# Attention kernel of two layers: which transpositions stand ahead of the output projection's portions, and in which parts a batch's normalisation is prepared

## What is computed

```python
xn = layernorm(x)
q, k, v = xn @ Wq + bq, xn @ Wk + bk, xn @ Wv + bv        # 16 heads of 64
q, k = rope(q), rope(k)
attn = softmax(causal(q @ k.T / 8))                       # 512 x 512 for each head
x = x + (attn @ v) @ Wo + bo + int8_linear(xn)            # attention + quantised linear layer
xn = layernorm(x)
left, right = xn @ compare_left, xn @ compare_right
c = left @ right.T / 16
x = x + ((c > threshold) * softmax(c + gate_bias)) @ xn + rwkv_ffn(xn)
```

## Time and profile before

| | us |
|---|---|
| median of 3 runs | 1048.55 |
| lowest, highest | 1047.62, 1048.55 |
| the profiled execution's time | 1048.61 |
| its span on the core | 1046.8 |
| PE busy | 997.9 (95%) |
| DVE, ACT, POOL busy | 846.8, 758.2, 766.6 |

### The profile page before, as it was taken

The page is one execution under the profiler, slowest core; times in us unless marked ns, Lnnn a source line. Parts: engine busy times, 40 slices in busy tenths (PEclk is TensorE's granted clock), DMA queues, the critical chain, the costliest instruction groups (busy, mean ns, idle before and its releaser), DMA issues.

```text
span 1046.8 us, 23671 instructions
## 1 busy us (share of the span) xinstructions
PE 997.9 (95%) x7974; PEld 673.3 (64%) x7974; DVE 846.8 (81%) x2272; ACT 758.2 (72%) x2014; POOL 766.6 (73%) x941
## 2 busy tenths in 40 slices
PE   5878998999999999999999999999999998999998
PEld 4545555666666666666666666666666765777776
DVE  7979889877878888877787777877787766998875
ACT  5968887666666767766666676666666766999994
POOL 3766667868787877787787878777867645878884
PEclk9989999999999999999999999999999999999999
DMA  8723444343333343234333333433333100000101
GB/s 273 231 82 112 142 132 134 92 132 92 111 108 92 97 117 99 90 114 119 92 92 111 92 97 91 122 97 91 99 101 96 52 1 1 22 22 21 34 30 41
DMA packets 99703, 98.70 MB, mean 94 GB/s; under 512 B 13312, under 2 KB 95360, under 8 KB 98944
## 3 DMA queue, kind: packets, MB, share of 16 engines
q1 hardware_dynamic: 99584, 97.19, 30.4%
HBM read 56.25 MB, written 40.90 MB: 93 GB/s over the span
## 4 chain that ended last, share of the span: by engine, by line
PE 71%; DVE 15%; ACT 7%; issue 4%; POOL 2%; DMA 1%; ACTq 0%; DVEq 0%; SPq 0%; POOLq 0%
PE bank L1640 22%; PE bank L1723 13%; PE bank L1737 12%; PE bank L1754 7%; PE bank L1711 6%; PE bank L1712 5%; PE bank L1929 2%; ACT arena L869 2%; PE bank L1875 1%; DVE arena L1516 1%; POOL arena L628 1%; DVE arena L1362 1%; DVE arena L1378 1%; DVE arena L1340 1%; DVE arena L1342 1%
## 5 line engine op out<-in xcount | busy, mean ns | idle before, releaser
L628 POOL TENSOR_SCALAR arena<-arena,rc 128x128 f32<-128x128 f32 (+3 forms) x512 | 275.4, 556 | 198.2 <-DVE rc L1371 198.2
L869 ACT ACTIVATE arena<-arena,nm 128x256 f32<-128x256 f32 (+3 forms) x512 | 283.4, 554 | 74.5 <-DVE nm L1362 69.1
L1362 DVE CUSTOM_DVE_ANT_0 arena<-bank,mask_rows 128x256 f32<-128x256 f32 (+3 forms) x512 | 232.9, 482 | 79.0 <-PE bank L1712 78.4
L1723 PE MATMUL bank<-ident,arena 128*128 128x128 f32 x1280 | 222.7, 280 | 20.1 <-DVE arena L1378 14.4
L1723 PEld LDWEIGHTS bank<-ident,arena 128*128 128x128 f32 x1280 | 149.1, 140 | 87.6 <-DVE arena L1378 52.1
L877 ACT ACTIVATE arena<-bank 128x512 f32<-128x512 f32 (+3 forms) x256 | 108.5, 424 | 65.6 <-PE bank L1723 65.5
L1737 PE MATMUL bank<-arena 128*64 128x512 f32 (+3 forms) x1024 | 153.1, 441 | 0.0
L1712 PE MATMUL bank<-arena 128*128 128x256 f16 (+3 forms) x512 | 152.9, 299 | 0.0
L1711 PE MATMUL bank<-arena 128*128 128x256 f16 (+3 forms) x512 | 139.9, 300 | 1.9 <-DMA arena<-scr 1.9
L1378 DVE COPY arena<-bank 128x512 f32<-128x512 f32 (+3 forms) x256 | 124.8, 487 | 20.6 <-PE bank L1723 16.8
L1737 PEld LDWEIGHTS bank<-arena 128*64 128x64 f32 x1024 | 68.1, 137 | 96.0 <-issue 71.6
(11 more groups left out here) (173 smaller groups left out, 2201.6 us busy)
## 6 DMA issues: line engine op xcount, KB each, us to landing
arena<-scr SPq DMA_DIRECT2D x320, 128.0 KB, 2.7
scr<-arena SPq DMA_DIRECT2D x256, 128.0 KB, 1.7
arena<-in_weights SPq DMA_DIRECT2D x5, 1024.0 KB, 7.5
x_sb<-in_x SPq DMA_DIRECT2D x8, 512.0 KB, 8.6
out<-x_sb SPq DMA_DIRECT2D x16, 256.0 KB, 2.2
xscr<-arena SPq DMA_DIRECT2D x12, 256.0 KB, 3.0
xsh<-xscr SPq DMA_DIRECT2D x6, 256.0 KB, 3.6
xsl<-xscr SPq DMA_DIRECT2D x6, 256.0 KB, 4.1
```

The costliest lines, as they stand in the source:

```text
L628: last = pool.tensor_scalar(pr[slot][:, OFF[i]:OFF[i + 1]], pr[slot][:, OFF[i]:OFF[i + 1]], rc[:, slot, i:i + 1], 1.0, ALU.mult, ALU.mult)
L869: act.activation(pr[slot][:, OFF[i]:OFF[i + 1]], pr[slot][:, OFF[i]:OFF[i + 1]], ACT.Exp, scale=-1.0, bias=nm[:, slot, i:i + 1], accum_out ...
L1362: dve.tensor_tensor_reduce(pr[slot][:, OFF[i]:OFF[i + 1]], s_tile[i], mask_rows[:, SQ - P * (i + 1):SQ], -1.0, -MASKED, ALU.add, ALU.min, ...
L1723: last = pe.transpose(banks[5 + h][:, (i - j) * P:(i - j + 1) * P], pr[2 * par + h][:, OFF[i] + j * P:OFF[i] + (j + 1) * P], ident[:])
```

## The change

Six edits, all of them in the order or the placing of instructions. No product is added or removed but for the fill.

1. PE: `pt(n, 0, 1)` goes ahead of `ffn`, `attended` and `columns_of_rows(n, 0)`; `pt(n, 2, 0)` and `pt(n, 2, 1)` go ahead of the second half's `attended` and `columns_of_rows(n, 1)`.
2. DVE: the roots of batches 1 to 7 are done in four parts: the first guess at the end of ring -1, steps 1 and 2 in the first gap of ring 0, step 3 with `roots_bias` and `bvs` in its second gap. The estimate lies in PSUM bank `wo` until the last step, and the step's three operations are written in another order, so that each reads it once.
3. DVE: `row_maximum(0)` goes to the end of ring 0, `row_maximum(1)` to the first gap of ring 1, the four `part_maximum` to rings 1 to 4, one each (before: rings 1 and 2 one each, ring 3 two); `column_maximum` and `weight_scale` of ring 5's second gap, `low_part(0..3)` and `quantise(0, 1..3)` of rings 8 to 10 go from the gaps to ring ends. ACT's `normal_rows(1)` in ring 0 is split like those of the later rings.
4. POOL: the memset of `kz[1]` goes behind the scaling of the tables.
5. PE: the 50 fill products of 128 columns ahead of ring -2's `evens` become 80 of 64 columns.
6. End: the last batch's last `av3` runs bank by bank, and the first `final` waits for the first bank alone.

```diff
--- POOL
             last.then_inc(diag_done, 1)
-            pool.memset(kz[1], 0.0).then_inc(kz_zero, 1)
 
             pool.wait_ge(setup_done, 1)
...
                 last.then_inc(tab_done, 1)
+            pool.memset(kz[1], 0.0).then_inc(kz_zero, 1)
--- ACT, ring
-                if 1 <= n < NB - 1:
+                if 0 <= n < NB - 1:
                     normal_rows(n + 1, (0,))
...
-                    normal_rows(n + 1, (2, 3) if n else range(NT))
+                    normal_rows(n + 1, (2, 3))
--- DVE
-            def root_step(s, base, r, y0, t1, t2):
-
-                dve.tensor_tensor(t2, y0, y0, ALU.mult).then_inc(s, 1)
+            def root_step(s, base, r, y0, t1, t2, out):
+
+                dve.tensor_tensor(t2, y0, t1, ALU.mult).then_inc(s, 1)
                 dve.wait_ge(s, base + 4 + 3 * r)
-                dve.scalar_tensor_tensor(out=t2, in0=t2, scalar=-0.5, in1=t1, op0=ALU.mult, op1=ALU.mult).then_inc(s, 1)
+                dve.scalar_tensor_tensor(out=t2, in0=t2, scalar=-0.5, in1=y0, op0=ALU.mult, op1=ALU.mult).then_inc(s, 1)
                 dve.wait_ge(s, base + 5 + 3 * r)
-                dve.scalar_tensor_tensor(out=y0, in0=t2, scalar=1.5, in1=y0, op0=ALU.add, op1=ALU.mult).then_inc(s, 1)
+                dve.scalar_tensor_tensor(out=out, in0=t2, scalar=1.5, in1=y0, op0=ALU.add, op1=ALU.mult).then_inc(s, 1)
...
             def first_gap(n):
 
-                if 0 <= n < NB and n != 1:
+                if n == 0:
+                    roots(later_tiles, 1, (1, 2), wo)
+                elif n < NB and n > 0:
                     row_maximum(n)
...
-                elif n == 8:
-                    low_part(0)
-                elif n == 9:
-                    quantise(0, 1)
-                elif n == 10:
-                    low_part(2)
...
                 elif n == 0:
-                    dve.wait_ge(act_stats, NB - 3)
-                    inverse_roots(slice(1, NB), 1)
+                    roots(later_tiles, 1, (3,), wo)
+                    roots_bias(later_tiles)
                     dve.tensor_scalar(bvs[:], vec[:, V_BV:V_BV + NP], inv[:, G_V:G_V + 1], None, ALU.mult)
-                elif 1 <= n <= 3:
-                    if n == 1:
-                        row_maximum(1)
+                elif 1 <= n <= 4:
                     part_maximum(n - 1)
-                    if n == 3:
-                        part_maximum(3)
-                elif n == 5:
-                    column_maximum(slice(G_O, G_L), 2)
-                    weight_scale(slice(G_O, G_L), 2)
+                elif n == 6:
                     dve.tensor_tensor(sc_vo[:], sc[:, G_V:G_V + 1], sc[:, G_O:G_O + 1], ALU.mult)
-                elif n == 8:
-                    low_part(1)
-                elif n == 9:
-                    quantise(0, 2)
-                elif n == 10:
-                    low_part(3)
...
             def ring_end(n):
 
-                if n == 7:
+                if n == 0:
+                    row_maximum(0)
+                elif n == 5:
+                    column_maximum(slice(G_O, G_L), 2)
+                    weight_scale(slice(G_O, G_L), 2)
+                elif n == 7:
                     quantise(0, 0)
+                    low_part(0)
                 elif n == 8:
                     input_scale()
+                    low_part(1)
                 elif n == 9:
-                    quantise(0, 3)
+                    for step in range(1, 4):
+                        quantise(0, step)
+                elif n == 10:
+                    low_part(2)
+                    low_part(3)
...
                 odd_terms(n + AHEAD)
+                if n == -1:
+                    dve.wait_ge(act_stats, NB - 3)
+                    roots(later_tiles, 1, (0,), wo)
                 inverse(n + 1, 1, e)
--- PE, ring
                 scores(n + 1, 0, (0, 2))
+                pt(n, 0, 1, o)
                 if n == NP + 2:
                     ffn(0, 0, wo)
...
                 if 1 <= n < NB:
                     columns_of_rows(n, 0)
-                pt(n, 0, 1, o)
                 scores(n + 1, 0, (3,))
...
                 scores(n + 1, 1, (1,))
+                pt(n, 2, 0, o)
+                pt(n, 2, 1, o)
                 if n == NP + 2:
                     attended(0, 0, (0, 1, 2), wo)
...
                     columns_of_rows(n, 1)
-                pt(n, 2, 0, o)
-                pt(n, 2, 1, o)
                 scores(n + 1, 1, (0, 2))
--- PE, fill and end
-            FILL = (0, 60, 0, 50)
+            FILL = (0, 60, 0, 40)
+                for _ in range(count):
+                    for a, z in ((identb, maskb), (maskb, identb)):
+                        pe.matmul(pt1[:, 0:L], a[:], z[:, 0:L], start=True, stop=True)
...
+            def av3_by_bank(n, j, par):
+
+                after(pe, pt3l_done, made(4, n, j))
+                for w in range(2):
+                    av3_terms(j, par, (2 * w, 2 * w + 1)).then_inc(av3_mm, 1)
```

## The result

The changed kernel takes 1032.74 us in the median (1031.76 to 1034.57), against 1048.1 for the kernel before measured beside it: a ratio of 0.9856, with an interval of 0.9838 to 0.9873. Forecast was 1028.0, a gain of 20.6; the gain is 15.4.

The account below looks back on a forecast made before the run. PE paces the rings, so a step saves time only where PE waits or runs at a low clock. From 1048.6, -11.2 + 0.5 - 5.05 - 3.35 - 0.8 - 0.7 = -20.6 gives 1028.0 us, range 1024.8 to 1032.8.

Parts of the forecast that it names:

- The steady wait: Rings 12 to 59: transpositions ahead of the projection remove PE's wait for DVE's copy; -11.2 us, bounds 0 and 17 saved.
- rival (a): Saving given back at the next copy: the wait at pt(n,3,1) grows from 0.14 to 0.39; 1039 us, chance 0.07.
- The other 44 save 0.25: Of the 48 rings from 12 to 59, all but rings 25 to 28 save 0.25 us each, 11.0 in sum.
- rival (c): In 52 rings the projection gets stuck behind POOL's normalise(n,1) at pt(n,0,1); slower, 1065 us, chance 0.03.
- Rings 60 to 63: Waits of 0.1 to 0.75 for POOL's normalise at pt(n,0,1), against 0.25 saved in each; +0.5 us in sum.
- Moving `pt(n,2,h)` 0.65 ahead: Needs ACT's copy of key tile 1; costed at nothing, gain only 0.04 us in rings with n % 4 == 0.
- Ring 0 and the start: Roots in parts and PE's clock staying up, -5.05 us; faster first root and weight maxima at the start, -0.8.
- the hidden guess: The roots' first guess at ring -1's end, hidden where DVE waits 0.9 us for ACT's sums and POOL is idle.
- Rival (b) in its second form: Ring 0's clock falls at 1.5 us of idling all the same, +2.6; 1030.6 us, chance 0.22 for either form.
- The memset beside the low parts: POOL's memset beside Wq's low parts at the start costs nothing, since it only writes SBUF; upper bound 1.8 us.
- Rings 1 to 9: DVE work moved out of gaps shortens PE's waits; -3.35 us including rings 10 and 11, bounds -1.5 and -4.5.
- The end: First bank's six products and final need not wait for the other bank's six; -0.7 us, bounds 0 and -0.8.

Follow-up runs that it names:

- `first_only`: The changed kernel with pt(n,2,0) and pt(n,2,1) back behind the projection's portion, pt(n,0,1) still ahead; 1031.91 us, ratio 0.9847.
- `pe_only`: The kernel before with the PE order alone changed (both moves of the transpositions), nothing else; 1040.01 us, ratio 0.9927.
- `roots_sbuf_b`: The changed kernel with the roots' estimate in SBUF instead of PSUM, same four places, second run for a clean profile; 1034.75 us, ratio 0.9872.
- `after`: The changed kernel itself, with all six edits, against the kernel before; 1032.74 us, ratio 0.9856.
- `second_only`: The changed kernel with pt(n,0,1) back behind the projection, pt(n,2,0) and pt(n,2,1) still ahead; 1043.16 us, ratio 0.995.

## Why the prediction was off by 4.7

By the profiled executions the forecast was off by 5.1, in these parts.

- **The steady wait, -11.2 forecast, -9.1 found.** The mechanism was right: 0.24 in most rings with n % 4 not 0 (12.43 to 12.19), from the first move alone, with the next copy shifting along, so rival (a) fell. The step that failed is the count: "The other 44 save 0.25", with 0.4 taken off for rings with one-off work. Rings 20, 23, 58 and 59 gave nothing and ring 22 gave 0.17; in rings 23 and 58 the wait at `pt(n,3,1)` comes from DVE's one-off work, and it grew by as much as was saved (ring 58: from 0.52 to 0.81 by the spacing of the products). Ring 59 has no `evens` any more and belongs with the next item. Ring 29 lost 0.23, since POOL's normalise was late in it and the projection stood behind: rival (c) in one ring. The ten rings with n % 4 == 0 gave 0.22 and not 0.29. I had taken 0.4 off for all this; it is 2.5.
- **Rings 60 to 63, +0.5 forecast, +2.06 found.** Here the failed step is "Moving `pt(n,2,h)` 0.65 ahead ... I cost it at nothing". I had checked ACT's copy in a ring with `evens`. In rings 59 to 63 no `evens` stand between the transpositions of tile 1 and those of tile 2, only scores and the projection, and the second move takes the projection out of the way too. So PE comes to tile 2 before ACT's and DVE's copies of tile 1 are done (in ring 61 the loads wait 0.31 and 0.20, in ring 60 PE itself 0.30): 1.6, shown by `first_only`. The +0.5 for POOL's normalise was right (0.45).
- **Ring 0 and the start, -5.85 forecast, -6.02 found.** The waits of `roots_bias` and `bvs`, the hidden guess and the clock that stays up at a short wait came as worked out, and from the V product to ring 1 it is 19.13 - 14.17 = 4.96 less, for the 5.05 forecast. PE's wait was 0.77, below the 1.5 forecast. That the sum agrees within 0.2 is in part luck on both sides. The maxima ended 1.2 earlier and not 0.8, and the first stretch of the changed kernel is 68.3 to 71.3 in the twelve profiles with the roots in parts and in PSUM, all with the same DVE work in ring 0. And 1.0 of the 4.96 is the long fall in the profile of the kernel before, as `pe_only` shows; I read one execution's fall as the kernel's. Rival (b) in its second form (the clock falls at 1.5 of idling) didn't come true in ring 0. The falls at the two earlier waits cost 0.1 to 1.0 and not its 2.6.
- **The memset beside the low parts.** It cost nothing (4.48 and 4.48), so the rule of the Trainium skill ("SBUF — State Buffer", section "Who interferes with whom"), that two SBUF inputs contend with a GpSimd instruction that reads SBUF and not with one that only writes it, agrees with the trace. The trace agrees for readers too: 0.84 to 0.91 beside the scaling of the tables, and Newton steps of 0.4 to 1.2 in SBUF beside normalise and `rotate` against 0.19 with one operand in PSUM. Two steps with SBUF inputs at the start of normalise took 0.18 and 0.19 all the same; why isn't shown.
- **Rings 1 to 9, -3.35 forecast with rings 10 and 11, -2.72 found.** Rings 3, 4 and 5 went as forecast (-0.58, +0.60, -1.36), and rings 8 and 9 too (-1.14 for -1.2). Ring 1 gave 1.12 and not 0.6, which hid most of the next miss. Ring 6's +0.68 was missed: I read the `sc_vo` move as a cost of nothing. A DVE operation on two SBUF columns has no cost of its own worth booking, but waits out the POOL instruction beside it, which is what the forecast said of `roots_bias` and failed to say here. Ring 10 lost 0.34, in waits for normalise at `pt(10,0,1)` (0.33 by the spacing of the products, more than the 0.25 saved) and for ACT at `pt(10,2,0)` (0.25; without the second move, in `first_only`, the ring loses 0.06).
- **The end, -0.7 forecast, +0.28 found.** The 0.65 came at the finals and the first store, and 0.47 at the second; the landing took them back (from 2.2 to 3.1 for the slowest). The step that failed is that the end of the span follows the last store's issue at a fixed distance.

## What to carry to other kernels

Moving a step ahead of filler work gains what its follower waited, and it must be checked in every kind of ring, above all in the last ones where the filler or the following work is missing; a sum over "all rings" by the most frequent one's rows was 2 us too good. A one-column operation with both inputs in SBUF can cost the rest of the POOL instruction beside it (0.67 here) and not its own time (0.13), so it belongs where its engine waits and POOL is idle. When a kernel's executions scatter, put the falls of the clock beside the times of all executions before blaming them: here the slowest had none, and the profiles show that the landing of a DMA moved more.

## What the runs showed of the hardware

- Newton steps on 28 columns with both inputs in SBUF took 0.40, 0.52 and 0.63 beside POOL's TENSOR_SCALARs and 1.21 beside a TENSOR_TENSOR of 1.26, and 0.18 to 0.19 with one input in PSUM (`roots_sbuf_b`, `after`).
- A one-input TENSOR_SCALAR on 4 columns took 2.06 beside a POOL memset of 1.80, while eight two-input operations took 4.48 with the same memset beside them and without it; those of them beside POOL's TENSOR_SCALARs took 0.84 to 0.91 each, those beside the memset 0.47.
- The granted clock fell to half (0.51 to 0.53, the 1.2 GHz level) after PE waits of 2.04 to 3.11 in the first 60 us, and not after waits of up to 1.91, in fifteen profiles of fourteen kernels. The length of the one wait doesn't decide it: at 851.9 us of `second_only` it fell (0.50) behind waits of 1.20 and 0.16, and in the kernel before it didn't behind waits of 1.20 and 0.26 at the same place.
- Stores of 256 KB landed in 2.1 to 2.4 in the three profiles in which the last two were issued 0.78 apart, and the slowest in 2.8 to 4.0 in all twelve in which the last two were issued 0.97 apart.
